# A four-layer graph network on Trainium2: layer 0 computed as (A x) W, with the rows of x as stationary operand, its product begun beside the transposes, and its row sums moved to ScalarE

## The reference

```python
# layer 0, per element
deg = sum(adj, axis=-1)                      # row sums, 1024
agg = (adj @ x) / max(deg, 1e-6)             # 1024x256
out = relu(concat([x, agg]) @ W.T)           # W: 256x512
x = layernorm(x + out)
# layer 1: three hops over A * exp(leaky_relu(s_j + s_i)), normalised by rows
# layer 2: three convolutions adj @ (x W) + b
# layer 3: attention, 8 heads of 32, scores scaled by 2*adj
```

## Time and profile before

| what | value |
|---|---|
| median of the runs | 3095.44 us (3094.74 to 3097.22) |
| the profiled execution | 3097.23 us |
| its span (first to last instruction) | 3095.4 us |
| mean granted TensorE clock | 0.991 of full |
| busy: PE, PEld, DVE, ACT, POOL | 2983.7, 2603.0, 2102.9, 1753.6, 452.2 us |
| PE share of the chain that ended last | 88% |

### The profile page before, as it was taken

One profiled execution on the slowest core, in us unless ns is written; L12 is line 12 of the kernel. 1 busy time (PEld: TensorE's weight loads), 2 busy tenths in 40 slices (PEclk: granted clock), 3 DMA queues, 4 the chain that ended last, 5 costly groups with the idle time before them and its releaser, 6 DMA issues.

```text
span 3095.4 us, 70348 instructions
## 1 busy us (share of the span) xinstructions
PE 2983.7 (96%) x27740; PEld 2603.0 (84%) x27740; DVE 2102.9 (68%) x4100; ACT 1753.6 (57%) x3119; POOL 452.2 (15%) x1666
## 2 busy tenths in 40 slices
PE   6999999999999999999999999999999999999999
PEld 5987789877898788987889877898778987889877
DVE  4637976379762897628976389753887548874488
ACT  3536855368552684527854378543784337853387
POOL 0101211012110121101211012111121111211112
PEclk8999999999999999999999999999999999999999
DMA  6022131121321213202133021330213302133110
GB/s 221 29 82 71 45 147 54 58 71 44 146 71 45 67 53 137 89 30 67 50 137 110 12 72 43 137 110 15 69 52 128 110 21 66 50 127 109 39 29 19
DMA packets 145268, 234.45 MB, mean 76 GB/s; under 512 B 12839, under 2 KB 113964, under 8 KB 144940
## 3 DMA queue, kind: packets, MB, share of 16 engines
q1 hardware_dynamic: 144940, 229.96, 23.1%
HBM read 120.86 MB, written 83.89 MB: 66 GB/s over the span
## 4 chain that ended last, share of the span: by engine, by line
PE 88%; DVE 6%; ACT 3%; issue 2%; POOL 1%; SPq 0%; DVEq 0%; DMA 0%; POOLq 0%; ACTq 0%
PE ps L531 17%; PE ps L533 16%; PE ps L532 16%; PE ps L762 15%; PE ps L752 10%; PE ps L780 8%; DVE t_lo L1284 1%; PE ps L630 1%; DVE qk L1587 1%; PE ps L793 1%; PE ps L620 1%; ACT t_hi L971 1%; PE ps L589 1%; DVE u_lo L1326 1%; DVE xt_lo L1291 0%
## 5 line engine op out<-in xcount | busy, mean ns | idle before, releaser
L1606 DVE CUSTOM_DVE_ANT_0 r<-ps,adjn 128x1024 f32<-128x1024 f32 x512 | 620.6, 1212 | 25.3 <-DVE xr L1655 10.3
L1228 ACT ACTIVATE r<-r,nmax 128x1024 f32<-128x1024 f32 x512 | 584.9, 1142 | 27.5 <-POOL nmax L523 27.3
L531 PE MATMUL ps<-u_hi,t_hi 128*128 128x256 f32 x2048 | 589.1, 288 | 2.3 <-DVE t_lo L1284 1.7
L533 PE MATMUL ps<-u_hi,t_lo 128*128 128x256 f32 x2048 | 580.3, 283 | 0.0
L532 PE MATMUL ps<-u_lo,t_hi 128*128 128x256 f32 x2048 | 580.0, 283 | 0.0
L762 PEld LDWEIGHTS ps<-ident,r 128*128 128x128 f32 x4096 | 462.7, 141 | 114.1 <-issue 75.3
L762 PE MATMUL ps<-ident,r 128*128 128x128 f32 x4096 | 537.0, 274 | 3.6 <-DVE pt L1624 3.5
L1624 DVE COPY pt<-ps 128x512 f32<-128x512 f32 x512 | 353.0, 689 | 86.2 <-PE ps L762 74.4
L531 PEld LDWEIGHTS ps<-u_hi,t_hi 128*128 128x128 f32 x2048 | 391.9, 191 | 6.1 <-DVE t_lo L1284 6.1
L971 ACT ACTIVATE pt<-ps 128x512 f32<-128x512 f32 x512 | 304.0, 594 | 156.1 <-PE ps L762 155.5
L532 PEld LDWEIGHTS ps<-u_lo,t_hi 128*128 128x128 f32 x2048 | 391.8, 191 | 0.0
(11 more groups left out here) (171 smaller groups left out, 5074.8 us busy)
## 6 DMA issues: line engine op xcount, KB each, us to landing
adjn<-in_adj SPq DMA_DIRECT2D x64, 512.0 KB, 3.8
t_spill<-t_hi SPq DMA_DIRECT2D x64, 512.0 KB, 5.7
t_spill<-t_lo SPq DMA_DIRECT2D x64, 512.0 KB, 5.8
t_hi<-t_spill SPq DMA_DIRECT2D x32, 1024.0 KB, 5.4
t_lo<-t_spill SPq DMA_DIRECT2D x32, 1024.0 KB, 8.2
xn<-in_x SPq DMA_DIRECT2D x16, 512.0 KB, 4.6
x_spill<-xn SPq DMA_DIRECT2D x64, 128.0 KB, 1.7
q_stack<-u_hi SPq DMA_DIRECT2D x64, 128.0 KB, 2.4
```

The lines of the kernel that those rows point to most:

```text
L531: pe.matmul(dst, a_hi, b_hi, start=first, stop=False, skip_group_check=check)
L533: return pe.matmul(dst, a_lo, b_hi, start=False, stop=last, skip_group_check=check)
L1228: act.activation(r[:, s % RSLOTS, :], r[:, s % RSLOTS, :], ACT.Exp, bias=nmax[:, s % 4:s % 4 + 1], accum_out=prow[:, qt % 2, h:h + 1]).the ...
L1606: dve.tensor_tensor_reduce(out=r[:, s % RSLOTS, :], in0=ps[:, 2 * (s % 2):2 * (s % 2) + 2, :].rearrange("p a c -> p (a c)"), in1=adjn[:, q ...
```

## The change

In layer 0 the product is regrouped: first A x is summed for all of one half of the rows (transposed: 256 features by 512 rows), then multiplied by the weight.

- x needs no product first: ScalarE rounds it straight from SBUF into `u_hi` (`x_rounded`, 4 copies of 512), VectorE takes the rest (`x_rest`).
- `summed(j, ft, half)`: the rows of x (`uh`, `ul`) are stationary and the transposed adj moves, 512 columns at a time: 96 matmuls of 512 columns into banks 0 to 3. For half 0 they run j by j, as column tiles come, with the transposes of half 1, of x, and four own parts written between them (table `BESIDE_0`); half 1 runs ft by ft with the other own parts and the rows 0 to 3 between (`BESIDE_1`).
- `aggregated`: the sums are rounded to `xt_hi`, `xt_lo` in the place of the transposed x (so ScalarE waits for the own parts that read it); `aggregated_row(t)` is then 6 matmuls of 256 columns.
- Own parts go to a place for all eight tiles, `own`.
- `degree` moves from VectorE to ScalarE as a Copy of 128x1024 with an accumulated output, into a new tile `unread`; `s_i` writes its unused product there too.
- At the end of an element the last tile's statistics (VectorE) and the last `normalise` (ScalarE) move behind the first units of the next element; all of adj's half 0 is transposed first.

```diff
-    TP_L0 = ([("adj", j, half) for half in range(HALVES) for j in range(TPH)] + x_units(0, 0) + adj_units(4, 5) +
-             x_units(0, 1) + adj_units(6, 7))
+    second = lambda *js: [("adj", j, 1) for j in js]
+    TP_L0 = ([("adj", j, 0) for j in range(NT)] + second(0, 1, 2, 3) + x_units(0, 0) + second(4) + x_units(0, 1) +
+             second(5, 6, 7))
+    BESIDE_0 = {0: (("adj", 1),), 1: (("adj", 2),), 2: (("adj", 3), ("x", 0)), 3: (("adj", 4),), 4: (("x", 1), ("own", 0)),
+                5: (("adj", 5), ("own", 1)), 6: (("adj", 6), ("adj", 7)), 7: (("own", 2), ("own", 3))}
+    BESIDE_1 = {(0, 0): (("own", 4), ("own", 5)), (0, 2): (("row", 0),), (0, 4): (("own", 6), ("own", 7)),
+                (0, 6): (("row", 1),), (1, 1): (("row", 2),), (1, 3): (("row", 3),)}
...
+                def summed(j, ft, half):
+
+                    pe.wait_ge(tp_free, nth(b, TP_UNITS, tp["adj", j, half] + 1))
+                    at = slice(half * 512, (half + 1) * 512)
+                    last = three(ps[:, ACC + 2 * half + ft, :], uh[:, j, ft * P:(ft + 1) * P], ul[:, j, ft * P:(ft + 1) * P],
+                                 t_hi[:, j, at], t_lo[:, j, at], j == 0, j == NT - 1)
...
+                def aggregated_row(t):
+
+                    if t >= 2:
+                        pe.wait_ge(acc_free, nth(b, 3 * NT, t - 1))
...
+                for j in range(TPH, NT):
+                    transpose_adj(b, j, 0)
+                transpose_adj(b, 0, 1)
+                for j in range(NT):
+                    pe.wait_ge(x_rows, nth(b, PAIRS, j // 2 + 1))
+                    for ft in range(FT):
+                        summed(j, ft, 0)
+                    beside(BESIDE_0[j])
+                pe.wait_ge(tp_free, nth(b, TP_UNITS, len(TP_L0) - 2))
+                for ft in range(FT):
+                    for j in range(NT):
+                        summed(j, ft, 1)
+                        beside(BESIDE_1.get((ft, j), ()))
+                transpose_x_half(b, 1, 0)
+                aggregated_row(4)
+                aggregated_row(5)
                 s_j(b, 0)
+                aggregated_row(6)
+                aggregated_row(7)
...
+                aggregated(b, 0)
+                own_part_0(b, (4, 5))
+                degree(b, (4, 5))
+                own_part_0(b, (6, 7))
+                degree(b, (6,))
+                normalise(b, 0, 0)
+                degree(b, (7,))
+                normalise(b, 0, 1)
+                act.wait_ge(agg_full, nth(b, 2 * FT, FT + 1))
+                normalise(b, 0, 2)
+                aggregated(b, 1)
+                normalise(b, 0, 3)
                 x_transposed(b, 1, 0)
+                normalise(b, 0, 4)
+                normalise(b, 0, 5)
...
+            def x_rest(b, pairs):
+
+                for k in pairs:
+                    if k == PAIRS - 1:
+                        dve.wait_ge(xr_free, b + 1)
+                    dve.wait_ge(x_hi, nth(b, PAIRS, k + 1))
...
+                aggregated(b, 1)
+                x_transposed(b, 1, 0)
+                for t in range(TPH, NT):
+                    layer_0_row(b, t)
+                    if t < NT - 1:
                         s_i(b, t - 2)
...
                         adj_transposed(b + 1, (0, 1), (0,))
-                        degree(b + 1, (0,))
```

More of the change, by code:

```diff
@@ L829, in _ @@
[L829 to L835, removed]
+                def summed(j, ft, half):
[3 more added lines that the diff above has]
+                                 t_hi[:, j, at], t_lo[:, j, at], j == 0, j == NT - 1)
+                    if j == NT - 1:
+                        last.then_inc(agg_full, 1)
@@ new lines, in beside @@
+                def beside(units):
+                    for kind, n in units:
+                        if kind == "adj":
+                            transpose_adj(b, n, 1)
+                        elif kind == "x":
+                            transpose_x_half(b, 0, n)
+                        elif kind == "own":
+                            own_part_0(n)
+                        else:
+                            aggregated_row(n)
+                for j in range(TPH, NT):
+                    transpose_adj(b, j, 0)
@@ L1047, in normalise, with x_rounded, own_part_0 @@
                                scale=rstd[:, t % 4:t % 4 + 1]).then_inc(ln_done, 1)
+            def x_rounded(b, pairs):
+                for k in pairs:
+                    act.wait_ge(x_in[k // 2], nth(b, 16, 16))
+                    copy(u_hi[:, k * 512:(k + 1) * 512], xn[:, 2 * k:2 * k + 2, :].rearrange("p t f -> p (t f)")).then_inc(x_hi, 1)
+            def own_part_0(b, ts):
+                for t in ts:
+                    n = pr["layer 0", t]
+                    act.wait_ge(pr_full, nth(b, PR_UNITS, n + 1))
+                    copy(own[:, t, :], ps[:, PR + n % 2, 0:F]).then_inc(pr_act, 1)
@@ new lines, in degree, with aggregated @@
+            def degree(b, js):
+                for j in js:
+                    act.wait_ge(adj_in[j], nth(b, 16, 16))
+                    if b or j:
+                        act.wait_ge(deg_sum, nth(b, NT, j))
+                    act.activation(unread[:, :], adjn[:, j, :], ACT.Copy,
+                                   accum_out=rsum[:, j:j + 1]).then_inc(deg_sum, 1)
+            def aggregated(b, half):
+                for ft in range(FT):
+                    n = FT * half + ft
+                    act.wait_ge(agg_full, nth(b, 2 * FT, n + 1))
+                    act.wait_ge(pr_full, nth(b, PR_UNITS, pr["layer 0", TPH * (half + 1) - 1] + 1))
+                    copy(xt_hi[:, ft, half * 512:(half + 1) * 512], ps[:, ACC + n, :]).then_inc(agg_act, 1)
@@ L1062, in _ @@
[L1062 to L1070, removed]
+                own_part_0(b, (0,))
```

177 lines of the change are left out of this document (94 added, 83 removed).

## The result

The changed kernel takes **3085.85 us** (3083.41 to 3087.20, 7 runs) where the kernel before, on the same chip, takes 3095.22 (3094.74 to 3097.32, 7 runs): a ratio of 0.9967, 95% interval 0.9956 to 0.9978.

A forecast was written before the change was run, and what follows sets the result against it. TensorE, busy 96%, was taken as the bound, with idleness and slow clock at element starts. -18.0 without the clock, -5.1 costlier starts, +13.6 clock: -9.5 from 3097.23 gives 3087.7, less 1.8 to the median: 3086 us; range 3070 to 3107.

The forecast's parts named there:

- costlier starts: Element starts: three cost 1.7 us more than element 1's in slow clock, which now goes too: -5.1 us.
- the clock: Behind the new wait at layer 0's end: clock falls, price 0 to 3.4 us, taken as 1.7: 8 x 1.7 = 13.6.
- element 0: Element 0, without such a start: first product at 47.4, late transposes at 95.0 against 94.1: +0.9 us.
- new idle stretch: End of layer 0: TensorE runs out of work by 469.5 and waits 3.3 us for the late transposes at 472.8.
- Work of TensorE: Layer 0 products: same columns in fewer, wider matmuls, 22.8 against 21.8 us: a gain of 1.0.
- start: Element start: 3.5 us wait goes, `c_f` 0.85 us sooner; x's load gates the first product at 425.2, idle some 1.7.
- middle: First product to last sum: 35.5 us of TensorE work, to 460.7, with banks free in time.
- The chain at the end: After the last sum: layer norm at 2.08 us a tile, tile 6 normalised at 472.1, late transposes at 472.8.
- rival 4: End of layer 0: layer norm of tiles 4 to 6 is no bound, 3.3 us more each, no fall: 3046; chance 0.05.
- rival 1: End of layer 0: the clock doesn't fall at the new wait: -23.1, 3072.3 us; chance 0.20.
- Rival 2: Clock falls for longer at the end and at the start too: +16, 3111.4 us; chance 0.14.
- Rival 3: Middle: in-order lists cost 1 us an element, through late x or a row sum: +8, 3094 us; chance 0.21.

The follow-up runs named there:

- e3: Changed kernel with 12 matmuls of 512 columns that nobody reads, put in TensorE's wait at the end of layer 0: 3075.73 us.
- e8: Changed kernel with x loaded in four pieces of 256 KB, each with its own semaphore, instead of two of 512 KB: 3082.09 us.
- e7: Changed kernel with one of each element's eight row sums, that of row tile 0, back on VectorE ahead of `c_f`: 3088.78 us.
- e6: Changed kernel with the same instructions at the end of layer 0 in another order on TensorE and VectorE: 3063.27 us.
- e4: Changed kernel with the last statistics and `normalise` put back ahead of the next element's units: 3108.52 us.
- e5: e1 with ScalarE's deferred `normalise` put two copies later, behind those of x's first transposed columns: 3066.96 us.
- e10: e6 and e8 together, with ScalarE's deferred `normalise` also put behind one more copy: 3059.69 us.
- e1: Kernel before, products in old order, with last statistics and `normalise` deferred behind the next element's first units and row sums on ScalarE: 3080.31 us.
- e2: Kernel before, old order, with only the last statistics and `normalise` deferred; row sums stay on VectorE: 3083.22 us.

## Why the prediction was right

The forecast of 3086 us met 3085.85 by its own mechanism; that it came so close is luck. In the spans of the profiled executions the forecast was -9.5 us and the result -12.1: the costlier starts gave 2.5 us less than forecast, the clock cost 4.3 less, and element 0 came out 1.0 better. The remaining 2.6 us vanish in the medians, because the profiled execution of before lies 2.0 us above its median and that of the changed kernel 0.5 below.

| step of the prediction | forecast | measured |
|---|---|---|
| first product, element 1, after the context's end | 5.9 us | 425.96 - 420.44 = 5.5 |
| idleness ahead of it | 1.7 in two pieces | 1.3 in two pieces |
| first product to last sum | 35.5 | 35.8 |
| wait for `normalise` of tile 3 | 1.4 | 1.18 |
| L621 after the last sum | 12.1 | 11.75 |
| new idle stretch | 3.3 | 3.05 |
| late transposes sooner, per element | 2.7 | 57.66 - 54.99 = 2.7; 3.1 in element 1 |
| element 0 | +0.9 | -0.1 |
| three costlier starts | -5.1 | -3 x 0.86 = -2.6 |
| clock behind the new wait | 8 x 1.7 = +13.6 | 8.9 + 0.3, and 10.1 by e3 |
| a row sum on ScalarE | 1.33 | 1.05 + 0.19 |

57.66 is the mean of the four starts before whose window read 0.83; the three that read 0.66 have a mean of 58.52. The forecast was read from element 1, the longest of the four (58.13).

- **Work of TensorE, start, middle, end.** All held within half a microsecond. The 512-column matmuls run at the distance read from the earlier trace rows, 0.23 us (eight from 459.52 to 461.36). That x's load becomes the gate is shown by e8 (0.56 us of a first piece that lands sooner reach TensorE). That the row sum held up `c_f` is shown by e7, but its 0.85 was not a gain of its own: with x behind it only some 0.6 counts. For all eight row sums together no run was made in the new order.
- **The chain at the end.** That the layer norm of tiles 4 to 6 bounds the end (against rival 4) is shown by e6, where the same instructions in another order bring L621 1.5 us nearer.
- **The clock, the step that failed in size.** In the profiled execution the fall came at eight of eight ends and at no start, as forecast, and rival 1 (3072 us) did not come. But e3 shows that it stood for something real: 3075.7 is what the change would give at full clock. The Trainium skill's page "TensorE: Matmul & The Clock Gate", section "What's actually happening", says that the transition point varies. The traces agree: in the changed kernel the slow stretch begins between 0.8 us before and 1.3 us after the transposes that end the wait. They show besides that it can fail to come: the same wait of 3.05 to 3.41 us was followed by a fall at 6 of 8 ends in e7, 7 of 8 in e8 and 3 of 8 in e4. The *size* was wrong, twice. I took half of the slow time as lost. The clock's records of the changed kernel give 34.1 us at 1.2 GHz at the eight ends (six of 3.41, two of 6.83), which would be 17 us; e3 finds 10.1. In the kernel before, the second 3.4 us of a fall cost 0.86 us and not 1.7. Element 1 shows three reasons. Its slow stretch begins at 472.7, while TensorE sits idle until 473.49. From there TensorE works without a pause, but not at half its pace:

```profile
475.05 0.42 PE L545 MATMUL ps<-w_lo,xt_hi 128*128 128x256 f32 x1
...
476.97 0.41 PE L545 MATMUL ps<-w_lo,xt_hi 128*128 128x256 f32 x1
```

Nine distances in 1.92 us are 0.213 us for 256 columns, against the 0.119 of the earlier trace rows: slow time full of work loses 0.44 of itself. And some of the loss is caught up behind it: TensorE's 30th matmul after the wait comes 2.7 us later than in e3 (6.28 against 3.62 us from the first late transpose), the 60th 2.1 us later (10.45 against 8.34), and 2.1 is what the second half is longer. What each of the three makes over all eight ends was not worked out.
- **Element 0**: the first product comes at 46.48, not 47.4. It stands behind six units and x's first rest, as forecast; it is the units that came sooner, since the clock was back at 2.4 GHz from 39.2 us on and not from 43.6 as in the kernel before. In e6, which has the same order here and the clock of before (0.53 over 26 to 44 us in both, 0.72 in the changed kernel), it comes at 47.24.
- **Rival 2** (a fall at both places) is what element 1 of e4 shows, but there the deferral is missing. **Rival 3** has no row: TensorE shows no wait in the middle.

What the prediction did not see is how the net splits. Its title change, the regrouping, brought next to nothing: e5 (old order) needs 53.99 us where the changed kernel needs 54.99 and pays 1.3 for the clock besides. The shorter work itself came; the waits ate it. Windows of TensorE over the first half of element 1 (window, us, busy (count), clock, DMA), changed kernel, then e5:

```profile
418.51:473.49 54.98, 49.20 (x368) 0.99 0.46 178
417.48:471.50 54.02, 50.21 (x465) 1.00 0.48 181
```

TensorE is busy 1.0 us less, as forecast, and idle 5.8 us instead of 3.8. Only with its end reordered (e6, 53.50) is the new order ahead, by 0.5 us. Since the old order's own end was not reordered, nor x loaded in four pieces there, which order is better at its best is open. The gain of the change as it stands hangs on the deferral.

## What to carry to other kernels

When a change moves several things, run each alone: here two moved calls carried the gain (e4), and the large regrouping cost some 19 us against the better old order (e5) until the work behind it was put in order too. A shorter product needs a look at what it used to hide: 48 matmuls of two row tiles had covered a layer norm. And where an engine with an in-order list must wait, what matters is not how long it waits but what stands behind it: 0.75 us less of such a wait changed nothing in one place (e10), and 1.3 us less, with the wanted copies ahead of it, made the kernel 13 us faster in another (e5).

## What the runs showed of the hardware

- Behind the same idle stretch of TensorE, 3.05 to 3.41 us at the end of layer 0, the granted clock of the profiled executions fell to 1.2 GHz at 24 of 32 ends (8 of 8 in the changed kernel, 7 in e8, 6 in e7, 3 in e4): likely, not certain. It fell behind none of e6's ends, where 1.45 and 0.45 us of idleness lie either side of 3 us of work. At the starts: in e1, with about 0.5, 0.4 and 1.94 us near each other, it fell at five of seven starts; in e2, with 0.96, 0.2, 0.57 and 1.94 us, at one of seven.
- At 1.2 GHz matmuls of 256 columns started 0.213 us apart against 0.119 at 2.4. A fall cost less than half its length: 0.9 to 1.5 us for 3.41 us and 2.0 to 2.1 for 6.83 (changed kernel against e3). Work that nobody reads, in a wait that can't be removed, pays for itself: 12 matmuls of 2.95 us in all made each element 1.3 us shorter.
- Of a load of 512 KB the first half can be had 1.3 us sooner as a load of its own (2.7 against 4.0 us to landing), and the last piece lands 0.4 us later: at 421.9 + 4.5, where the second half lands at 420.9 + 5.1.
